# Scratch of q and k with three terms a row, four loads a batch, and minus-maximum rows sent from ScalarE's queue

## The reference

```
q = layernorm(x) @ Wq.T + bq      k = ctx @ Wk.T + bk      v = ctx @ Wv.T + bv
attn = softmax(q k^T / sqrt(d))   x = x + tanh(g_xattn) * ((attn v) @ Wo.T + bo)
```

## Time and profile before

| | us |
|---|---|
| median of 3 runs | 882.24 (880.23 to 885.28) |
| the profiled execution | 883.96 |
| its span, first to last instruction | 881.5 |
| what lies around the span | 2.5 |
| PE / DVE / ACT / POOL busy in the span | 807.0 / 527.6 / 414.9 / 419.0 |

### The profile page before, as it was taken

One profiled execution on the slowest core, in us unless ns is written; L12 is line 12 of the kernel. 1 busy time (PEld: TensorE's weight loads), 2 busy tenths in 40 slices (PEclk: granted clock), 3 DMA queues, 4 the chain that ended last, 5 costly groups with the idle time before them and its releaser, 6 DMA issues.

```text
span 881.5 us, 19410 instructions
## 1 busy us (share of the span) xinstructions
PE 807.0 (92%) x7106; PEld 717.3 (81%) x7107; DVE 527.6 (60%) x1083; ACT 414.9 (47%) x687; POOL 419.0 (48%) x461
## 2 busy tenths in 40 slices
PE   2658999999999999888899999999999999999996
PEld 2645677767777777656799999999999999999995
DVE  4254679888999987874655443433333333246785
ACT  5324777767767676554333433333333433333331
POOL 3522333666656564337656164828564663226000
PEclk9566999999999998979999999999999999999998
DMA  4887899999999999224457632414232321217521
GB/s 136 161 156 135 169 185 181 191 263 196 196 190 198 192 179 193 80 82 149 141 183 208 238 115 72 143 48 138 68 117 59 124 66 48 72 49 303 208 93 51
DMA packets 101549, 127.36 MB, mean 144 GB/s; under 512 B 18672, under 2 KB 83440, under 8 KB 101488
## 3 DMA queue, kind: packets, MB, share of 16 engines
q1 hardware_dynamic: 87344, 80.37, 42.6%
q0 software_dynamic: 14144, 46.19, 15.6%
HBM read 75.36 MB, written 50.91 MB: 143 GB/s over the span
## 4 chain that ended last, share of the span: by engine, by line
PE 73%; DVE 11%; DMA 6%; issue 4%; SPq 3%; ACT 2%; POOL 0%; DVEq 0%; ACTq 0%
PE bank L518 8%; PE bank L520 7%; PE bank L519 7%; PE bank_sm L518 5%; PE bank_sm L519 5%; PE bank_sm L520 5%; PE bank_ss L518 5%; PE bank_ss L520 5%; PE bank_ss L519 5%; DVE row_max L1136 5%; PE bank L605 5%; PE bank_ss L576 4%; DMA qk_d<-qk_s 3%; PE bank_sm L589 3%; PE bank L612 2%
## 5 line engine op out<-in xcount | busy, mean ns | idle before, releaser
L1136 DVE TENSOR_REDUCE row_max<-bank_sm 128x4 f32<-128x1024 f32 x124 | 151.5, 1221 | 41.8 <-PE bank_sm L589 40.6
L863 ACT ACTIVATE probs_T<-bank_ss 128x1024 f32<-128x1024 f32 x123 | 126.4, 1028 | 31.6 <-PE bank_ss L576 24.0
L1115 DVE TENSOR_TENSOR gT_l<-gg,gT_h 128x1024 fp32r<-128x1024 f32 x50 | 68.9, 1378 | 88.3 <-ACT gT_h L982 88.2
L518 PE MATMUL bank<-w_h,gT_h 128*128 128x256 f32 x400 | 114.1, 285 | 6.0 <-DVE x_all L1409 3.2
L518 PE MATMUL bank_ss<-xg_h,w_h 128*128 128x256 f32 x400 | 115.9, 290 | 0.0
L518 PE MATMUL bank_sm<-xg_h,w_h 128*128 128x256 f32 x400 | 113.7, 284 | 1.5 <-DVE xg_l L1115 1.5
L519 PE MATMUL bank<-w_h,gT_l 128*128 128x256 f32 x400 | 113.7, 284 | 0.0
L520 PE MATMUL bank<-w_l,gT_h 128*128 128x256 f32 x400 | 113.4, 284 | 0.0
L519 PE MATMUL bank_sm<-xg_h,w_l 128*128 128x256 f32 x400 | 113.1, 283 | 0.0
L520 PE MATMUL bank_sm<-xg_l,w_h 128*128 128x256 f32 x400 | 113.0, 282 | 0.0
L520 PE MATMUL bank_ss<-xg_l,w_h 128*128 128x256 f32 x400 | 112.8, 282 | 0.0
(11 more groups left out here) (177 smaller groups left out, 2038.4 us busy)
## 6 DMA issues: line engine op xcount, KB each, us to landing
qk_d<-qk_s SPq DMA_DIRECT2D x32, 512.0 KB
w_raw<-wall POOLq DMA_DIRECT2D x27, 512.0 KB
k<-qk_d SPq DMA_DIRECT2D x96, 128.0 KB
q<-qk_d SPq DMA_DIRECT2D x96, 128.0 KB
xg<-xs_d SPq DMA_DIRECT2D x35, 257.0 KB
y_pairs<-y_d POOLq DMA_DIRECT2D x16, 512.0 KB, 9.4
x<-x SPq DMA_DIRECT2D x16, 256.0 KB
c_s<-ctxT SPq DMA_DIRECT2D x16, 256.0 KB, 3.3
```

The source lines that it names most:

```text
L518: pe.matmul(out, ah, bh, start=first and k == 0, stop=False)
L863: act.activation(pT[:, 2 * (pv % 4):2 * (pv % 4) + 2, :].rearrange("p h t -> p (h t)"), exp_bank(V.b, pv)[:, :], ACT.Exp, scale=D ** -0.5) ...
L1115: return v.tensor_tensor(dst, ps, high.bitcast(F32), ALU.subtract)
L1136: v.tensor_reduce(mx[B.slot][:, :, :].rearrange("p t (r q) -> p r t q", r=2)[:, :, :, p], max_bank(B.b, p)[:, :].rearrange("p (r t k) -> p ...
```

## The change

The scratch `qk_d` gets the shape (slot, side, chunk, partition, term, L): the three terms of a feature lie behind each other. `half_out` now waits for the high part alone and stores it twice, into its two terms, then waits for the low part and stores it once: three DMAs of 256 KB. `terms_in` loads all three terms of one head parity in one DMA over 48 partitions, two loads a side instead of six. The transposed maxima are sent by ScalarE's own queue, right behind the copy that makes them, and no longer by SyncE. Batch 0's maxima are transposed at the end of iteration -1 and not in step 0 of iteration 0. The x loads of the first 7 batches go to the head of SyncE's iteration and wait for one batch less of `var1_ok`; `x_in` becomes two semaphores in turn.

```
-        qk_d = nc.dram_tensor("qk_d", (R, 8, P, L), F32, kind="Internal").ap()
+        qk_d = nc.dram_tensor("qk_d", (R, 2, EC, P, 3, L), F32, kind="Internal").ap()
...
-                moved(sp, var1_ok, n.n())
+                moved(sp, var1_ok, n.n(1, -1))
...
             def half_out(A, side):
                 if A.b > 0:
-                    sp.wait_ge(qk_st[side], A.n(16))
-                for done in ((qh_ok, ql_ok), (kh_ok, kl_ok))[side]:
-                    sp.wait_ge(done, A.n(1, 1))
-                sp.dma_start(qk_d[A.slot, 4 * side:4 * side + 4].rearrange("c p t -> p c t"),
-                             qk_s[:, 4 * side:4 * side + 4, :].bitcast(F32)).then_inc(qk_st[side], 16)
+                    sp.wait_ge(qk_st[side], A.n(48))
+                sp.wait_ge((qh_ok, kh_ok)[side], A.n(1, 1))
+                for term in (1 - side, 2 - side):
+                    sp.dma_start(qk_d[A.slot, side, :, :, term, :].rearrange("c p t -> p c t"),
+                                 qk_s[:, 4 * side:4 * side + 2, :].bitcast(F32)).then_inc(qk_st[side], 16)
+                sp.wait_ge((ql_ok, kl_ok)[side], A.n(1, 1))
+                sp.dma_start(qk_d[A.slot, side, :, :, 2 * side, :].rearrange("c p t -> p c t"),
+                             qk_s[:, 4 * side + 2:4 * side + 4, :].bitcast(F32)).then_inc(qk_st[side], 16)
             def terms_in(F, side):
...
-                    for first, terms, half in (((0, 1, 1), (1, 2, 0)), ((0, 2, 0), (2, 1, 1)))[side]:
-                        c8 = 4 * side + 2 * half
-                        rows = qk_d[F.slot, c8:c8 + 2].rearrange("c p t -> (c p) t")
-                        rows = rows.rearrange("(s q d) t -> q d s t", q=2, d=D)[par]
-                        for term in range(first, first + terms):
-                            r0 = ROWS * par + D * term
-                            dst = (q4, k4)[side][F.slot][r0:r0 + D, :, :]
-                            sp.dma_start(dst.bitcast(F32), rows).then_inc(stk[F.slot], 16)
+                    rows = qk_d[F.slot, side].rearrange("c p n t -> (c p) n t").rearrange("(s q d) n t -> q d n s t", q=2, d=D)[par]
+                    rows = rows.rearrange("d n s t -> (d n) s t")
+                    dst = (q4, k4)[side][F.slot][ROWS * par:ROWS * par + 3 * D, :, :]
+                    sp.dma_start(dst.bitcast(F32), rows).then_inc(stk[F.slot], 16)
...
-                if C:
-                    sp.wait_ge(mT_ok, C.n(1, 1))
-                    for par in range(2):
-                        row = ROWS * par + MROW
-                        sp.dma_start(q4[C.slot][row:row + 1, :, :].bitcast(F32), mT[8 * par:8 * par + 8, :].bitcast(F32)).then_inc(mrow, 16)
+                if X and among_first(X, RX):
+                    load_x(X)
...
-                    if p == 0 and C:
...
+                    if p == 0 and C and not among_first(C, 1):
+                        turn_max(C, S2)
...
+                if B and among_first(B, 1):
+                    turn_max(B, None)
...
                         act.activation(mT[:, :], mT_p, ACT.Copy, scale=-1.0).then_inc(mT_ok, 1)
+                        act.wait_ge(mT_ok, C.n(1, 1))
+                        for par in range(2):
+                            row = ROWS * par + MROW
+                            act.dma_start(q4[C.slot][row:row + 1, :, :].bitcast(F32), mT[8 * par:8 * par + 8, :].bitcast(F32)).then_inc(mrow, 16)
```

More of the change, by code:

```diff
@@ L265, in build @@
         zero_ok = sem("zero_ok"); q_zero = sem("q_zero"); k_init = sem("k_init"); v_init = sem("v_init"); gate_ok = sem("gate_ok"); bo_ps = sem("bo_ps"); gbo_ok = sem("gbo_ok")
-        x_in = sem("x_in"); c_in = sem("c_in")
+        x_in = [sem(f"x_in{i}") for i in range(2)]; c_in = sem("c_in")
         var1_ok = sem("var1_ok"); rstd1_ok = sem("rstd1_ok"); var2_ok = sem("var2_ok"); rstd2_ok = sem("rstd2_ok")
@@ L345, in load_x @@
             def load_x(n):
-                moved(sp, var1_ok, n.n())
-                sp.dma_start(x_s[n.x_slot][:, :, :], x[bass.ds(n.b, 1)].rearrange("b (t p) d -> p (b t) d", p=P)).then_inc(x_in, 16)
+                moved(sp, var1_ok, n.n(1, -1))
+                sp.dma_start(x_s[n.x_slot][:, :, :], x[bass.ds(n.b, 1)].rearrange("b (t p) d -> p (b t) d", p=P)).then_inc(x_in[n.b % 2], 16)
             def load_c(n):
@@ L369, in half_out @@
                 if A.b > 0:
-                    sp.wait_ge(qk_st[side], A.n(16))
-                for done in ((qh_ok, ql_ok), (kh_ok, kl_ok))[side]:
-                    sp.wait_ge(done, A.n(1, 1))
-                sp.dma_start(qk_d[A.slot, 4 * side:4 * side + 4].rearrange("c p t -> p c t"),
-                             qk_s[:, 4 * side:4 * side + 4, :].bitcast(F32)).then_inc(qk_st[side], 16)
+                    sp.wait_ge(qk_st[side], A.n(48))
[6 more added lines that the diff above has]
+                             qk_s[:, 4 * side + 2:4 * side + 4, :].bitcast(F32)).then_inc(qk_st[side], 16)
             def terms_in(F, side):
-                sp.wait_ge(qk_st[side], F.n(16, 16))
+                sp.wait_ge(qk_st[side], F.n(48, 48))
                 if among_first(F, R):
@@ L417, in one @@
                     store_x2(S2)
-                if X:
+                if X and not among_first(X, RX):
                     load_x(X)
@@ L583, in scores_to_max @@
                 if p == 0:
-                    pe.wait_ge(stk[B.slot], B.turn * 192 + 192)
+                    pe.wait_ge(stk[B.slot], B.turn * 64 + 64)
                 moved(pe, mx_ok, B.n(PAIRS, p - among_first(B, 1)))
@@ L634, in project_rows, with turn_max @@
                       lambda k: (high[:, k, :], rest[:, k, :]), EC).then_inc(done, 1)
+            def turn_max(C, S2):
+                pe.wait_ge(mx_ok, C.n(PAIRS, PAIRS))
+                if S2:
+                    pe.wait_ge(oTl_ok, S2.n(1, 1))
+                else:
+                    moved(pe, xnTl_ok, min(NB, C.n(1, 3)))
+                for qc in range(TC):
+                    r = pe.transpose(mT_p[:, qc * P:(qc + 1) * P], mx[C.slot][:, qc, :], ident)
+                r.then_inc(mT_ps, 1)
             def turn_out(S):
@@ L895, in q_or_k @@
                         act.wait_ge(ps, A.n(2, 2))
-                        moved(act, qk_st[side], A.n(16))
+                        moved(act, qk_st[side], A.n(48))
                     for half in range(2):
@@ L1239, in behind @@
                     if p == 0 and Eb:
-                        v.wait_ge(x_in, Eb.n(16, 16))
+                        v.wait_ge(x_in[Eb.b % 2], 16 * (Eb.b // 2) + 16)
                         stats(x_s[Eb.x_slot], bst)
```

## The result

The changed kernel takes 909.11 us (median of 4 runs, 905.78 to 912.76) for 882.45 of the kernel before beside it: ratio 1.0321 (95%: 1.0284 to 1.0358), 27 us slower. The forecast was 889, range 867 to 904. The direction was right, the size was not. The profiled execution took 911.37 us, its span is 909.4 at a mean granted clock of 0.942 (before 0.952).

What follows compares the result with a forecast made beforehand. TensorE, busy 807.0 of 881.5 us, was taken as the bound. Start -11, q loads -1, net stall +14.5 and clock +6 summed to +8.5 on 883.96; with the start's gain rounded up, 882.2 + 6.8 = 889, range 867 to 904.

Steps and rivals of the forecast that it cites:

- Issue on ScalarE, 1.47 us an iteration in the way of TensorE: Iterations 1 to 14: two DMA issues ahead of pair 6's exponentials delay them 1.47 us each, 20.6 us in all.
- Less what is given back: Later in the iterations: TensorE's 6.0 us of waits for VectorE absorb part of the 20.6 us stall, net +14.5.
- The clock: three falls, +6: Iterations 3 to 12, gap ahead of the router logits: three clock falls, +6 us, bounds 0 and +25 for ten.
- the rival of 904: Gap ahead of the logits from iteration 3 on: clock falls in nearly every iteration, +22 us, 904; chance 0.16.
- The sign by which the forecast said it would be wrong: Steady state: forecast wrong if the distance from iteration 2 to 12 grows under 8 us or over 35.
- The start, -11: Batch 0's second scores at about 62 us for 73.27, 11 us off the start, bounds 5 and 17.
- Rounds of loads, 8.25 to 9.1 us: Start-up rounds of stores and loads: 8.25 us, near 0.9 more with x or a context, against 9.1 and 10.5.
- The maxima's own queue: Start: batch 0's maxima, sent by ScalarE with no 786 KB ahead in their queue, land near 60.8 us.
- The 9 by that rule: Start: if another queue only saves issue time, the maxima land 2 or 3 us later, winning 9 for 11.
- x loads, early: Start: x of batches 2 to 6 sent before the k loads removes VectorE's wait of 6.88 us.
- q loads, -1: Steady state: TensorE's 0.9 us wait for q loads goes, as fewer bytes pass through few partitions, -1 us.
- the rest, nothing: Steady state: context, k and q loads go out some us sooner, for tiles wanted an iteration later, worth nothing.

Runs made afterwards that it cites:

- e2: The kernel before, with only the maxima's two DMAs moved to ScalarE's queue behind the copy: 917.47 us, ratio to before 1.0431.
- e9: The kernel before, with an extra unused copy on ScalarE behind the maxima's copy in iterations 1 to 12, no DMA moved: 903.84 us, ratio to before 1.0277.
- e3: The changed kernel with 14 unused filler matmuls on TensorE ahead of step 1's second scores, in iterations 1 to 12: 894.48 us, ratio to before 1.0154.
- e1: The changed kernel with the maxima's two DMAs issued by SyncE again, at the head of its iteration: 875.93 us, ratio to before 0.9949.
- e4: The changed kernel with the maxima's DMAs issued by ScalarE behind the exponentials of S's pair 6: 882.38 us, ratio to before 1.0024.
- e7: The changed kernel with the 16 rows of maxima sent in one DMA for two, still on ScalarE's queue: 882.14 us, ratio to before 1.0029.
- e8: The changed kernel, but only batch 0's maxima sent by ScalarE and all others by SyncE, in two DMAs: 870.58 us, ratio to before 0.9867.
- e11: The changed kernel, only batch 0's maxima sent by ScalarE, the rest by SyncE, in one DMA for two: 868.46 us, ratio to before 0.9873.
- e10: The kernel before with early x loads, batch 0's maxima turned in iteration -1 and sent by ScalarE, others by SyncE: 870.70 us, ratio to before 0.9906.
- e12: As e11, but with the old scratch and its six loads a side: 868.74 us, ratio to before 0.9840.
- e5: The kernel before with only the early x loads and the two semaphores they need: 878.63 us, ratio to before 0.9958.

## Why the prediction was wrong

Point by point, by its own steps:

- *Issue on ScalarE, 1.47 us an iteration in the way of TensorE.* Right: 628 ns an issue (640 taken), the exponentials 1.55 us later, TensorE's wait 1.94 us (1.83 forecast). e2 and e9 show it alone.
- *"Less what is given back": 6 us.* **Wrong, the first term that failed.** TensorE's waits for VectorE did shrink (7.5 us from 79 to 390 us before, 2.5 after), but with the clock held up (e3) twelve iterations still lose 19.6 us, where 12 x 1.55 is 18.6. The 19.6 holds one fall of the clock, for 3.4 us, and a wait of 1.45 us for the maxima, so that at most some 2 us came back, of the 5 that I had taken for as many iterations. The waits shrank only where the clock was low: e3, in the stretch in which the kernel before has 7.5 us of them and the changed one 2.5, has 5.9. VectorE's row maxima wait for the scores that stand behind the gap, so it moves with TensorE, as its own waits show (35.2 to 67.1 us). I treated time that VectorE owed as if it could be repaid. Over fourteen iterations the term is 22 for 14.5.
- *The clock: three falls, +6.* **Wrong, the larger term that failed.** The clock fell in thirteen of the fourteen iterations. The falls that the filler takes away, ten of the eleven in iterations 1 to 12, cost 14.6 us by the medians and 16.6 by the traces, some 1.7 each. The evidence for three was that 176 to 198 us held 2.15 us of idle time without a fall. That was idle time in many pieces. The new gap is 1.9 to 2.6 us in one piece. The nearer row, though it is but one gap, was the second of the earlier trace rows, a single gap of 1.64 us and half clock behind it. I also tied the falls to the router logits and so to iterations 3 to 12; they came without logits too, in iterations 1 and 2. This was the rival of 904, with a chance of 0.16: its mechanism (falls in nearly every iteration) is what happened, and its price of 20 for ten was a little high; what it lacked was the stall that did not come back. With 22 for the stall and 15 for the clock the same sum gives -12 + 22 + 15 = +25 for the 26.7 measured; these two are measured values put in, so this only adds up and tests nothing. (The recorded sum gives 890.7 on the median of 882.2; the 889 took 1.7 more off for a better start, away from what came.) The sign by which the forecast said it would be wrong (iteration 2 to 12 longer by less than 8 or more than 35 us) did not catch this: it grew by 30.3, inside bounds that had to hold the rival of 904 too.
- *The start, -11.* Nearly right: 9.6. The second scores of batch 0 came at 63.52 for the 62 forecast (73.27 before). How near is in part luck: in the traces of seven kernels with the same instructions up to there (the changed kernel, e1, e3, e4, e7, e8, e11) batch 0's copy lies between 54.98 and 59.28, which is 6.3 to 10.6 us earlier than before.
- *Rounds of loads, 8.25 to 9.1 us.* They took 9.0 to 9.5. The round from 30.38 to 39.37, less 1.25 fixed and 2.6 for the stores, leaves 5.1 us for 786 KB: 153 GB/s by my working, 127 before, within the bounds and slower than the middle I took. Not foreseen was that the first loads go 2.25 us earlier. Only 0.6 of it is the change's: the last store, now of 256 KB, is followed by the loads 2.35 us after its issue for 2.98. The rest stands ahead of any store: ScalarE began the first high parts at 15.61 for 17.17, and e9, which has the instructions of the kernel before there, began them at 15.76. The 153 rests on the forecast's rate for stores, which no run checks. Of the whole, e10 and e12 against e8 and e11 leave nothing that can be told.
- *The maxima's own queue.* It did not bring them sooner over the engines: from the issue of the second to TensorE's start are 5.92 us for 6.07 before, and TensorE waited 3.27 us for them, as much as before. They had been forecast to land near 60.8. What the queue saves is the time until they are issued: 0.4 us behind the copy for 4.6 in e1, and second scores at 63.52 for 66.44. The Trainium skill's page "DMA: Bandwidth & Descriptors", section "Issuing engines are not separate DMA queues", says that all queues share the same 16 engines and another one saves issue time only. This trace agrees, in its 5.92 us for a transfer of 8 rows that had only its twin ahead of it in its queue. The 9 by that rule was nearer to the 9.6 than my 11, but both lie inside the 6.3 to 10.6 or at its edge, and one trace can't choose between them.
- *x loads, early.* Right, and the surest part: VectorE's wait of 6.88 us is gone, and e5 alone is 0.9958 of before (0.9928 to 0.9989).
- *q loads, -1, and the rest, nothing.* The q loads don't stand among the waits after; whether that is worth anything beside the stall can't be told. From batch 15 to the end it was 0.9 us less, but in the traces of all kernels this part varies from 495.7 to 503.2.

## What to carry to other kernels

A DMA that is moved to another engine's queue is an instruction of that engine. Look at the next one behind it: if the bottleneck waits for that one already (here 0.36 us), each microsecond of issue is paid in full, and more if the gap it opens takes the clock down. Judge the risk to the clock by single gaps, not by the idle time of a stretch: here 26 of 30 gaps of 1.9 us and more took it down, and 6 of the 14 of 1.12 to 1.55 us in e7. And use the other queue only where the transfer would wait in its own: here for one batch of sixteen, where it brought the scores 3.4 to 4.3 us closer to the copy.

## What the hardware showed

- A DMA of 8 rows, one target row, takes ScalarE 628 ns to issue and SyncE 640; one for all 16 rows takes 0.50 us, less than one of the two.
- More work on TensorE made the kernel 14.6 us faster (e3). The clock fell at 26 of 30 single gaps of 1.9 to 2.6 us (changed kernel, e2, e3), with router logits behind them or not, at 7 of 12 of 1.58 us (e9) and 6 of 14 of 1.12 to 1.55 (e7), and never between 84 and 360 us in e11, where that wait is at most 1.3 us.
- By an estimate from rounds in one trace each, which takes the stores at the forecast's 305 GB/s, loads of the same bytes moved at 153 GB/s over 48 partitions in 2 DMAs, and at 127 over 16 partitions in 6. The kernel gained nothing by it that can be told.
